# A four-layer graph network on one core: first chunk of edges inside the first layer, second layer's features added by TensorE, places brought first

## The reference, cut to what matters

```python
edge_index = jnp.stack([src, dst])                      # 100000 edges, sorted by dst
h = relu(layernorm(x))
x = x + L0(h, src, dst)       # Q[src].K[dst] per head, softmax over the heads, segment_sum of V[src]
h = relu(layernorm(x))
x = x + L1(h, edge_index)     # Chebyshev, K=3, twice: prop(h) = zeros.at[row].add(w * h[col])
h = relu(layernorm(x))
x = x + L2(h, edge_attr_64)   # see below
h = relu(layernorm(x))
x = x + L3(h)                 # attention over incoming edges

def L2(h, edge_feats):
    message = relu(h[dst] + edge_feats)                 # per edge, 64 wide
    reduced = segment_sum(message, src)                 # onto src
    y = (1 + eps) * h + reduced
    return relu(layernorm(y @ W1 + b1)) @ W2 + b2
```

## Time and profile before

| what | value |
| --- | --- |
| median of 3 runs | 4082.64 us (4072.29 to 4088.93) |
| the profiled execution | 4078.07 us |
| its span | 4076.3 us |
| PE busy | 1936.6 us (48%), 16923 matmuls |
| DVE busy | 2238.4 us (55%) |
| ACT busy | 1209.9 us (30%) |
| POOL busy | 1592.5 us (39%) |
| PE's granted clock, mean | 0.697 |

### The profile page before, as it was taken

The page is one execution under the profiler, slowest core; times in us unless marked ns, Lnnn a source line. Parts: engine busy times, 40 slices in busy tenths (PEclk is TensorE's granted clock), DMA queues, the critical chain, the costliest instruction groups (busy, mean ns, idle before and its releaser), DMA issues. The chain is left out here.

```text
span 4076.3 us, 62411 instructions
## 1 busy us (share of the span) xinstructions
PE 1936.6 (48%) x16923; PEld 1342.4 (33%) x16923; DVE 2238.4 (55%) x4872; ACT 1209.9 (30%) x3818; POOL 1592.5 (39%) x1665
## 2 busy tenths in 40 slices
PE   5835544454444444330223249992211255655377
PEld 4623333333333333220111126661111245545222
DVE  6876766666676776430211013323211399997899
ACT  1154444444444444230001002100000133334744
POOL 0055555555555555456766640006667400000000
PEclk8966666666666666665555569995555598896599
DMA  8611111111111111542222210004443222221000
GB/s 277 249 42 40 40 40 40 40 40 40 40 40 40 40 40 40 172 124 55 59 52 53 52 34 1 0 11 138 136 115 102 61 75 83 74 82 42 0 0 8
DMA packets 399312, 266.91 MB, mean 65 GB/s; under 512 B 321473, under 2 KB 349310, under 8 KB 399090
## 3 DMA queue, kind: packets, MB, share of 16 engines
q1 hardware_dynamic: 306278, 87.81, 10.1%
q10 hardware_dynamic: 41488, 118.96, 8.1%
q0 software_dynamic: 51488, 59.40, 6.0%
HBM read 158.59 MB, written 107.47 MB: 65 GB/s over the span
## 5 line engine op out<-in xcount | busy, mean ns | idle before, releaser
L1229 POOL DMA_INDIRECT sorted_edges<-r_load,r_to x800 | 792.0, 990 | 736.3 <-DMA r_to<-places 439.6
L805 POOL DMA_INDIRECT hsrc<-h,edges x808 | 778.4, 963 | 693.5 <-PE ps L998 460.1
L873 DVE TENSOR_TENSOR prod<-ps,hsrc 125x1024 f32<-125x1024 f32 x200 | 245.0, 1225 | 323.3 <-remote 180.1
L996 PE MATMUL ps<-blank 128*64 128x160 bf16 x101 | 31.5, 312 | 590.2 <-remote 579.3
L1401 PE MATMUL ps<-R,w_work 128*128 128x64 bf16 x3000 | 145.1, 206 | 272.3 <-DVE R L1743 148.2
L1537 ACT ACTIVATE R<-w_work 128x384 bf16<-128x384 f32 (+1 forms) x160 | 85.8, 536 | 617.6 <-DVE w_work L1733 506.5
L1733 DVE TENSOR_TENSOR w_work<-ps,w_work 128x384 f32<-128x384 f32 (+1 forms) x160 | 91.2, 570 | 306.3 <-remote 296.6
L1391 PE MATMUL ps<-R 128*128 128x64 bf16 x3000 | 142.9, 208 | 225.5 <-issue 132.7
L1331 PE MATMUL ps<-R,A 128*128 128x192 bf16 x1250 | 183.0, 267 | 138.8 <-issue 136.0
L864 DVE TENSOR_SCALAR hot<-ramp,small 125x400 bf16<-125x400 int16 x800 | 219.6, 326 | 49.9 <-issue 47.7
L952 ACT ACTIVATE lo<-ramp,edges 125x128 bf16<-125x128 int16 x808 | 246.8, 387 | 0.0
(11 more groups left out here) (414 smaller groups left out, 4419.4 us busy)
## 6 DMA issues: line engine op xcount, KB each, us to landing
w_work<-sorted_edges ACTq DMA_DIRECT2D x42, 1000.0 KB
sorted_edges<-A ACTq DMA_DIRECT2D x25, 1000.0 KB, 7.3
r_load<-in_edge_attr_dram SPq DMA_DIRECT2D x80, 312.5 KB
dstrow<-dst_rows SPq DMA_DIRECT2D x101, 234.4 KB
counts<-A ACTq DMA_DIRECT2D x5, 4000.0 KB, 30.2
A<-counts SPq DMA_DIRECT2D x12, 1600.0 KB
sorted_edges<-A ACTq DMA_DIRECT2D x3, 5000.0 KB, 28.7
hsrc<-h,edges POOLq DMA_INDIRECT x808
```

What stands on the lines that cost most here:

```text
L805: g.indirect_dma_start(out=hsrc[:, s, t, :], out_offset=None, in_=S.h0[:, :], in_offset=bass.IndirectOffsetOnAxis(ap=edges.bitcast(I32)[:, ...
L873: v.tensor_tensor(prod[0:TP, :].rearrange("p (t h f) -> p t h f", t=HT, h=H), S.ps[0:TP, hf * 1024:(hf + 1) * 1024].rearrange("p (t h f) - ...
L1229: g.indirect_dma_start(out=S.sorted, out_offset=bass.IndirectOffsetOnAxis(ap=to[:, hf, t:t + 1], axis=0), in_=load[:, hf, t, :], in_offset ...
```

## The change

Three things change.

The first chunk: SP waits for the clearing of `sorted`, clears the list's tail and brings both halves of chunk 0 ahead of its loop in `attend`. POOL scatters chunk 0 in `attend`, behind its last gather. Behind its last item SP waits for those scatters and brings chunk 1. The semaphores `sc` and `ready` are shared by both functions now, and the loops in `spread` begin at chunk 1. With it, DVE's order in an item of `attend` changes: top, subtraction and AO come ahead of the counts and of the projection's addition. The matrix of counts is stored in five parts for each block in place of two (`k=5`, 640 columns), and the sums of the first layer are added in the middle of the transposition groups, not ahead of them.

The second layer's features: PE multiplies the features (f32) by the identity into the bank in which the gathered rows are added (`features`), so `x` goes. ACT's L1537 and DVE's L1737 read that bank (`gathered`). The lowest part of a step is taken by DVE at the start of the next step (`lowest_of`).

`bring_half` issues the places first.

```diff
@@ bring_half
+    sp.dma_start(S.to[:, hf, :], S.pos[:, bass.ds(c * TC + hf * HALF, HALF)]).then_inc(S.landed[hf], 16)
     sp.dma_start(S.load[0:TP, hf, :, 0:D], I["edge_attr_64"][bass.ds(c * CE, CE), :].rearrange(by_edge, t=TC)[:, part, :]
...
-    sp.dma_start(S.to[:, hf, :], S.pos[:, bass.ds(c * TC + hf * HALF, HALF)]).then_inc(S.landed[hf], 16)
@@ attend, sync
             n = pairs_of(sp)
+            sp.wait_ge(S.cleared, 16 * S.clears)
+            r = sp.value_load(S.ovn[0:1, 2:3], min_val=0, max_val=E)
+            sp.dma_start(S.sorted[bass.ds(r + OVB, P), :], S.zrow[0:ROW].unsqueeze(0).to_broadcast([P, ROW])).then_inc(S.tail, 16)
...
+            sp.wait_ge(S.padded, 1)
+            for hf in range(2):
+                bring_half(nc, I, S, sp, 0, hf)
             with sp.Fori(0, n) as j:
...
-            sp.wait_ge(S.cleared, 16 * S.clears)
-            r = sp.value_load(S.ovn[0:1, 2:3], min_val=0, max_val=E)
-            sp.dma_start(S.sorted[bass.ds(r + OVB, P), :], S.zrow[0:ROW].unsqueeze(0).to_broadcast([P, ROW])).then_inc(S.tail, 16)
-            sp.wait_ge(S.padded, 1)
-            for hf in range(2):
-                bring_half(nc, I, S, sp, 0, hf)
             g, b = begin(n * 2, 0)
             line(g, n * 2)
+            for hf in range(2):
+                sp.wait_ge(S.sc[hf], 16 * HALF)
+                sp.sem_inc(S.ready, 1)
+                bring_half(nc, I, S, sp, 1, hf)
@@ attend, gpsimd, behind the loop
+            g.wait_ge(S.tail, 16)
+            for hf in range(2):
+                g.wait_ge(S.landed[hf], 48)
+                g.sem_inc(q["carrier"], 1)
+                for t in range(HALF):
+                    g.indirect_dma_start(out=S.sorted, out_offset=bass.IndirectOffsetOnAxis(ap=S.to[:, hf, t:t + 1], axis=0),
+                                         in_=S.load[:, hf, t, :], in_offset=None).then_inc(S.sc[hf], 16)
@@ attend, vector
+                    own.settle(summed)
+                    v.wait_ge(q["summed"], 2 * i + 4)
+                    own.step(v.tensor_reduce(top, s4, AX.X, ALU.max))
+                    v.tensor_tensor(s4, s4, over(top, [TP, T, H]), ALU.subtract).then_inc(q["soft"], 1)
                     v.sem_inc(q["spot_free"], 1)
                     v.wait_ge(q["hot"], T * i + T)
                     v.sem_inc(q["edges_free"], 1)
                     place(own, i + 1, 1 - s, j * 16 + 16 + 16 * s)
-                    own.settle(summed)
-                    v.wait_ge(q["summed"], 2 * i + 4)
-                    topped = own.did(v.tensor_reduce(top, s4, AX.X, ALU.max))
-                    v.wait_ge(q["counted"], i + 1)
-                    add_counts(0)
-                    own.settle(topped)
-                    v.tensor_tensor(s4, s4, over(top, [TP, T, H]), ALU.subtract).then_inc(q["soft"], 1)
-                    add_counts(1)
-                    v.wait_ge(q["proj"], i + 2)
-                    v.tensor_tensor(S.hpw[:, bass.ds(before, W)], S.hpw[:, bass.ds(before, W)], S.ps[0:D, 3584:3584 + W],
-                                    ALU.add).then_inc(q["proj_free"], 1)
...
                                     a4.unsqueeze(3).to_broadcast([TP, T, H, SUB]), ALU.mult).then_inc(q["ao"], 1)
+                    v.wait_ge(q["counted"], i + 1)
+                    add_counts(0)
+                    add_counts(1)
+                    v.wait_ge(q["proj"], i + 2)
+                    v.tensor_tensor(S.hpw[:, bass.ds(before, W)], S.hpw[:, bass.ds(before, W)], S.ps[0:D, 3584:3584 + W],
+                                    ALU.add).then_inc(q["proj_free"], 1)
@@ spread
-    counts = S.A.rearrange("p (b k n) -> p b k n", b=NB, k=2)
+    counts = S.A.rearrange("p (b k n) -> p b k n", b=NB, k=5)
     AFTER = 23
+    MIDDLE = len(groups) // 2
+    def gathered(k, m):
+        return S.bank[2 + k][:, 0:m * D].rearrange("p (b f) -> p b f", f=D)
...
-            with sp.Fori(0, AFTER) as c:
+            with sp.Fori(1, AFTER) as c:
                 both(c)
...
-            g.wait_ge(S.tail, 16)
-            with g.Fori(0, C2) as c:
+            with g.Fori(1, C2) as c:
@@ spread, tensor and vector: the 25 transposes and their additions become bring_sums() and add_sums(), called in
             for n, (i, j, c) in enumerate(groups):
+                if n == MIDDLE:
+                    bring_sums()
@@ second layer, tensor
+            def features(n, s):
+
+                pe.matmul(S.bank[2 + n % 2][:, 0:size(n) * D], S.ident[:, :], es[:, s, cols_of(n), 0:D], start=True, stop=False,
+                          skip_group_check=True)
...
                         pe.wait_ge(qm["oht"], i * GN + n + 1)
+                        features(n, s1)
                         for b in range(size(n)):
                             for d in range(SP3):
                                 mm = pe.matmul(S.bank[2 + k][:, b * D:(b + 1) * D],
-                                               ohT[:, k, b * P:(b + 1) * P], hw[:, s1, d, :], start=(d == 0), stop=(d == SP3 - 1))
+                                               ohT[:, k, b * P:(b + 1) * P], hw[:, s1, d, :], start=False, stop=(d == SP3 - 1),
+                                               skip_group_check=True)
...
-                        pe.wait_ge(qm["low"], i * GN + n + 1)
+                        pe.wait_ge(qm["low"], i * GN + n + 2)
@@ second layer, scalar
-                        act.wait_ge(qm["x"], i * GN + g + 1)
-                        nc.scalar.activation(mp[:, k, 0:m, 0, :], msg[:, k, 0:m, :], ACT.Relu).then_inc(qm["hi"], 1)
+                        act.wait_ge(qm["hg"], i * GN + g + 1)
+                        nc.scalar.activation(mp[:, k, 0:m, 0, :], gathered(k, m), ACT.Relu).then_inc(qm["hi"], 1)
@@ second layer, vector
+            def lowest_of(n, ahead):
+
+                k, m = n % 2, size(n)
+                v.wait_ge(qm["mid"], ahead + 1)
+                v.tensor_tensor(mp[:, k, 0:m, 2, :], msg[:, k, 0:m, :], mp[:, k, 0:m, 1, :], ALU.subtract).then_inc(qm["low"], 1)
...
-                        v.wait_ge(qm["hg"], i * GN + n + 1)
-                        v.tensor_tensor(msg[:, k, 0:m, :], S.bank[2 + k][:, 0:m * D].rearrange("p (b f) -> p b f", f=D),
-                                        es[:, s, cols, 0:D], ALU.add).then_inc(qm["x"], 1)
+                        lowest_of((n - 1) % GN, i * GN + n)
                         there(1 - k, n + 1, i * GN)
                         v.wait_ge(qm["hi"], i * GN + n + 1)
-                        v.scalar_tensor_tensor(msg[:, k, 0:m, :], msg[:, k, 0:m, :], 0.0, mp[:, k, 0:m, 0, :], ALU.max, ALU.subtract
+                        v.scalar_tensor_tensor(msg[:, k, 0:m, :], gathered(k, m), 0.0, mp[:, k, 0:m, 0, :], ALU.max, ALU.subtract
                                                ).then_inc(qm["rem"], 1)
...
-                        v.wait_ge(qm["mid"], i * GN + n + 1)
-                        v.tensor_tensor(mp[:, k, 0:m, 2, :], msg[:, k, 0:m, :], mp[:, k, 0:m, 1, :], ALU.subtract).then_inc(qm["low"], 1)
```

57 lines of the change are left out of this document (33 added, 24 removed).

## The result

The changed kernel took 4119.2 us (median of 20 runs, 4074.08 to 4169.85) against 4086.19 us for the kernel before (20 runs, 4069.74 to 4103.57). The ratio is 1.0066, with a 95% interval of 1.0044 to 1.0089: slower by 0.66%. The forecast was 4067 us, 0.4% faster, in a range of 4018 to 4112; the time is outside it and on the other side. The profiled execution of the changed kernel took 4122.45 us (span 4120.6), 44 more than that of the kernel before. The runs of the changed kernel spread over 96 us, those of the kernel before over 34. The ratios in this document leave out runs more than 1.5% above the fastest of their kernel, here four of the changed kernel's 20 (4136.52 to 4169.85), two of ten in e16_k5mid and one of ten in e14_k5places; the medians of all 20 runs would give 1.0081.

What follows compares the result with a forecast made beforehand. No engine full: POOL's gathers pace the first layer, its scatters slow the others between layers, DVE bounds the second loop. 4078 - 37 (loop) + 3 (items beside scatters) + 23 (between layers, barrier included) = 4067 us; range 4018 to 4112.

Steps and rivals of the forecast that it cites:

- The first layer: First layer: gather(0) 10.4 us later, at 230; DVE's new order worth 0; barrier at about 1727, 34 us later.
- The loop: Second layer's loop: 12.7 us per item in place of 13.8, over 34 items, -37 us (0 to -61).
- ACT's sum of 12.4 us per item: Second layer's loop: ACT's register loads and transfers set the steps, 12.4 us per item; 0.3 added for 1.2 GHz stretches.
- my 3.0 at full clock: Second layer's loop: PE's added f32 identity work takes 3.0 us per item at full clock, 5.8 at half.
- The two rivals in which its clock stays low: Second layer's loop: unchanged at 13.8 us per item (4104 us, chance 0.15), or bound by PE (4240 us, 0.05).
- the 65 ns of the Trainium skill: Second layer's loop: L1737 reading PSUM would grow by 65 ns, 9 us in all; the forecast put it at nothing.
- The step that failed: Between the layers: +23 us (0 to +38), the barrier's 34 included, as one chunk fewer behind it gives back 11.
- the small packets: Between the layers: the stores' 61 us of DMA queue time become 68 (up to 85).
- one price, 0.076 of a free us: Between the layers: each microsecond beside the scatters is worth 0.076 of a free one, from 7.01/92.46 busy us.
- the signs that I named for being wrong: Loop item over 13.5 or under 12 us, clock under 0.8, barrier off over 10, first-layer item moved over 0.15.
- Places first: SP's transfers: bringing places ahead of features costs 0, with 10 us either way in 38 chunks.
- The rival that nothing is given back: Between the layers: the moved chunk gives nothing back, the barrier's 34 us stay whole, 4078 us; chance 0.07.

Runs made afterwards that it cites:

- e16_k5mid: Kernel before with the new loop, small packets and the sums in the middle of the groups: 4105.82 us, ratio 1.0016.
- e14_k5places: Kernel before with the new loop, small packets and places first, in the session with the kernel before at 2883.19 us: 2884.4 us, ratio 0.9996.
- e4_move: Kernel before with the first chunk's move alone: 4124.33 us, ratio 1.0031.
- e2_loop: Kernel before with the second layer's new loop alone: 4066.49 us, ratio 0.9896.
- e1_k2: Changed kernel with the counts stored in two parts per block again (large packets): 4090.2 us, ratio 0.9942 to the kernel before.
- e3_k5: Kernel before with the counts stored in five parts per block alone (small packets): 4136.1 us, ratio 1.0062.
- e17_allhold: Changed kernel with chunk 2 brought only when all 84 groups are done: 4095.99 us, ratio 0.9968 to the kernel before.
- e10_places: Kernel before with the places brought first alone: 4125.8 us, ratio 1.0005.
- e18_k5places: Kernel before with the new loop, small packets and places first: 4135.19 us, ratio 1.0063.
- e9_noplaces: Changed kernel with the places brought last again: 4136.95 us, ratio 1.0036 to the kernel before.
- e5_nomove: Changed kernel without the first chunk's move: 4147.37 us, ratio 1.0084 to the kernel before.
- e8_noscatter: Kernel before without the 800 scatters, which POOL only reports done: 3257.07 us in a single run.
- e13: Kernel before with the new loop, small packets and sums in the middle, in the session with the kernel before at 2883.19 us: 2887.15 us, ratio 1.0015.
- e15: Changed kernel with chunk 2 held until all groups are done, in the session with the kernel before at 2883.19 us: 2905.13 us, ratio 1.0064.

## Why the prediction was wrong, point by point

- **The first layer** was right in each step. gather(0) came at 229.84 (forecast 230), the barrier at 1725.7 (1727). From gather(0) to the last item's first gather it took 1454.9 us, and 1461.5 - 5.9 = 1455.6 before: DVE's new order is worth nothing, as said. e4_move puts the whole move at +13 us (5 to 21 by its interval); the forecast for a barrier 34 us later with 11 given back, 23, is just above that.
- **The loop** was right in its mechanism and too careful in one term. ACT's sum of 12.4 us per item was the measured 12.43, with the step with the transfers at 3.17 in place of 2.9 and the wide one at 2.60 in place of 2.7; the 0.3 us that I laid on top for stretches at 1.2 GHz weren't there, as the clock rose from 0.89 to 1.00. The gain is 1.37 us per item, and 43 us in e2_loop, where 37 was forecast. PE's f32 work is 3.7 us per item (L1384 takes 1.02, 0.91, 0.89 and 0.89 us for the steps of one item), above my 3.0 at full clock, but PE is busy only 77% of the time. The two rivals in which its clock stays low fell with that. DVE's L1772 reads PSUM in 0.56 us, as L1737 read SBUF, so the 65 ns of the Trainium skill ("Perfetto Trace Analysis", section Optimizing Scalar/DVE Operations) aren't seen on DVE. On ScalarE the same section has PSUM cheaper by 42 ns, and the trace agrees in sign: 0.49 us for L1563 against 0.52.
- **The step that failed** is the one between the layers, in two terms. First, I priced the small packets by the time that the DMA queues take for them (61 us becoming 68) and let the groups run between the stores' landings. That price was right: the last store landed 68.0 us behind the barrier (62.3 before). What I put at nothing is ACT's issue: 45.8 us for the five stores in place of some 21, with three stalls among the groups (about 7, 12 and 10 us) where the kernel before had one of 6. Part of that comes from issuing them sooner: the same kernel with large packets has 31.6 us of issue (e1_k2), and what sets the groups back is that the last issue ends 48.1 us behind the barrier in the changed kernel and 37.9 in e1_k2. Some 70 us behind the barrier, when chunk 2 came, 42 groups were done in place of 64, and 62 in e1_k2. e3_k5 shows the cost alone, and e1_k2 takes it away.
- Second, I used one price, 0.076 of a free us, for everything beside the scatters. By the table it is 0.03 to 0.08 for the groups and about a third for the norms and degrees behind them. With one price it doesn't matter what is left when the scatters start; with two, the groups left are where the change loses its time: groups beside 426 us in place of 239, free time 427 in place of 345. That they are the place is shown by e17_allhold, which leaves none and is 0.98% faster. That it takes only 20 groups more is not: e3_k5 leaves as many and its free time is 360. The rest is in what each group takes there, 11.5 us against 7.5, and the cause of that stays open. A row of the kernel before would have told, the stretch right behind its last group, beside 7.01 us for 54 matmuls in 1800 to 1900:

```profile
2000.00:2100.00 100.00, 42.58 (x227) 19.90 (x227) 32.20 (x47) 5.61 (x11) 72.18 (x67) 0.67 0.26 60
```

42.58 us of PE and 32.20 of DVE beside as many scatters. I had taken the ratio from the one stretch. None of the signs that I named for being wrong lay in this stage.
- **Places first** at zero was right alone (e10_places) and not within the whole: with small packets and the loop it goes from -0.4% by the sum of the parts to +0.63% (e18_k5places). POOL's pauses would explain it (12 in place of 19 with them), and two kernels with small packets and the old order fit that, with 278 and 340 us for their 37 and 39 groups. e9_noplaces, also in the old order and with 18 pauses, hardly fits it: 455 us for 42, of which 50 are the sums', in the slowest of its ten runs. So how the order of SP's transfers acts stays open. The sums stand behind the 42nd group, just where small packets let the scatters begin. From the 42nd group to the next, 50 us went by in e9_noplaces and 24 in e5_nomove, but 3 in the changed kernel's profiled run.
- The rival that nothing is given back (4078) falls with e4_move: the barrier came some 31 us later there and the time grew by 13, not by 34. The prediction drew the same +34 from the Trainium skill ("Runtime: NRT & Kernel Launch", section Instruction fetch mechanics), by which fetch is mostly hidden; e4_move's 13 doesn't bear the 34 out, and no run shows whether fetch has a part in the slowness. e8_noscatter and the session of e13 to e15 show that the slowness needs the scatters, and isn't there in every session even with them.
- The spread of the changed kernel's runs (96 us) would fit many groups left to POOL's pauses; e17_allhold, where none are left, has 10 runs within 15 us. No run tested that by itself.

What stays open: by what way a scatter slows the other engines' instructions, why one of six sessions was free of it, and how the places' order and the small packets act together, which is part of why a group takes 7.5 us beside the scatters in one kernel and 14 in another.

## What to carry to other kernels

Before an edit is priced in a stretch where everything is slowed, ask which work will stand in it, and take a price for each kind: here one kind kept under a tenth of its pace and another a third. If an edit leaves more of the dear kind in it, one wait that holds the slowing traffic back can be worth more (1.0% on the changed kernel) than moving a fortieth of that traffic away, which alone cost 0.3%. And a store split into smaller packets is paid by the engine that issues it, so its issue belongs in the sum if that engine has other work behind it.

The version to keep is the kernel before with the new loop, without the chunk's move, the small packets and the sums in the middle: 1.04% faster alone, 1.34% with chunk 1 held, a difference between the two that isn't established.
